# Layer 1 attention: tail steps at new slots, maxima combined behind the last one, low halves of weights later, second batch's projections a tile sooner

## What is computed

```python
qkv = hidden_states @ Wqkv
q = qkv[..., :nH * d].reshape(B, S, nH, d)
k = qkv[..., nH * d:nH * d + d]
v = qkv[..., nH * d + d:]
scores = jnp.einsum('bqhd,bkd->bhqk', q, k) * scale
scores = jnp.where(causal[None, None], scores + alibi[None], NEG_INF)
probs = jax.nn.softmax(scores, axis=-1)
attn = jnp.einsum('bhqk,bkd->bqhd', probs, v).reshape(B, S, H)
return attn @ Wo
...
x = x + _layernorm(_L1_attn_ref(_layernorm(x, axis=-1), L1_attn_Wqkv, L1_attn_Wo), axis=-1)
x = x + _layernorm(_L1_ffn_ref(_layernorm(x, axis=-1), L1_ffn_sign, L1_ffn_scale), axis=-1)
```

## Time and profile before

| | us |
|---|---|
| median of 3 runs (4049.62 to 4056.49) | 4054.41 |
| the profiled execution's own time | 4068.57 |
| its span | 4066.7 |
| PE busy in the span | 3592.4 (88%) |
| DVE busy | 2894.3 (71%) |
| ACT busy | 2362.7 (58%) |
| POOL busy | 2083.7 (51%) |
| mean granted PE clock | 0.956 |

### The profile page before, as it was taken

One profiled execution on the slowest core, in us unless ns is written; L12 is line 12 of the kernel. 1 busy time (PEld: TensorE's weight loads), 2 busy tenths in 40 slices (PEclk: granted clock), 3 DMA queues, 4 the chain that ended last, 5 costly groups with the idle time before them and its releaser, 6 DMA issues.

```text
span 4066.7 us, 62815 instructions
## 1 busy us (share of the span) xinstructions
PE 3592.4 (88%) x21250; PEld 1803.7 (44%) x21250; DVE 2894.3 (71%) x4612; ACT 2362.7 (58%) x4071; POOL 2083.7 (51%) x1710
## 2 busy tenths in 40 slices
PE   3899998899888779999998999999999995776799
PEld 1344443233222345555554555555555553343344
DVE  4544336766674467888888888888888885657787
ACT  4533323555565566676676676666676663455665
POOL 4700000000000347777777877878778776546754
PEclk9999998899898899999999999999999997889999
DMA  3200001000100100000000000000000001012000
GB/s 104 66 10 1 1 21 28 1 7 13 37 8 4 36 18 1 25 13 21 19 8 25 8 26 13 14 25 1 26 13 20 11 1 65 1 52 78 13 11 32
DMA packets 58879, 88.92 MB, mean 22 GB/s; under 512 B 11429, under 2 KB 32440, under 8 KB 58548
## 3 DMA queue, kind: packets, MB, share of 16 engines
q1 hardware_dynamic: 57880, 84.15, 7.2%
q10 hardware_dynamic: 672, 0.59, 0.1%
HBM read 71.05 MB, written 6.85 MB: 19 GB/s over the span
## 4 chain that ended last, share of the span: by engine, by line
PE 62%; DVE 12%; issue 8%; ACT 6%; POOL 4%; SPq 1%; DVEq 0%; ACTq 0%; DMA 0%; POOLq 0%
PE psum L257 12%; PE psum L258 12%; PE psum L259 12%; PE psum L1397 3%; PE psum L1370 2%; PE psum L2495 2%; PE psum L2507 2%; PE psum L2503 2%; PE psum L2464 2%; DVE arena L1563 2%; PE psum L1381 2%; PE psum L3160 1%; PE psum L3161 1%; DVE x L2189 1%; PE psum L2486 1%
## 5 line engine op out<-in xcount | busy, mean ns | idle before, releaser
L257 PE MATMUL psum<-xt_hi,arena 128*128 128x512 f16 (+1 forms) x1920 | 739.4, 385 | 20.8 <-ACT arena L2017 5.9
L258 PE MATMUL psum<-xt_lo,arena 128*128 128x512 f16 (+1 forms) x1920 | 738.1, 384 | 0.0
L259 PE MATMUL psum<-xt_hi,arena 128*128 128x512 f16 (+1 forms) x1920 | 737.0, 384 | 0.0
L2290 POOL TENSOR_TENSOR arena<-arena 128x1024 f16<-128x1024 f16 x256 | 516.2, 2036 | 49.7 <-DVE arena L2101 32.4
L1563 DVE TENSOR_REDUCE arena<-psum 128x1 f32<-128x512 f32 (+3 forms) x608 | 373.5, 656 | 145.0 <-PE psum L1370 143.2
L257 PE MATMUL psum<-arena 128*128 128x512 f16 (+1 forms) x1152 | 420.2, 368 | 58.5 <-DVE arena L2925 25.5
L1512 ACT ACTIVATE arena<-psum 128x512 f32<-128x512 f32 x576 | 320.6, 599 | 244.9 <-PE psum L1381 161.2
L258 PE MATMUL psum<-arena 128*128 128x512 f16 (+1 forms) x1152 | 419.2, 367 | 0.0
L259 PE MATMUL psum<-arena 128*128 128x512 f16 (+1 forms) x1152 | 418.9, 367 | 0.0
L1311 POOL TENSOR_TENSOR rs<-sd,epsc 128x1 f32<-128x1 f32 x15 | 8.1, 540 | 785.0 <-DVE sd L1611 785.0
L2295 POOL TENSOR_TENSOR arena<-arena 128x512 f16<-128x512 f16 x256 | 314.6, 1248 | 4.6 <-PE psum L2475 4.6
(11 more groups left out here) (364 smaller groups left out, 8332.6 us busy)
## 6 DMA issues: line engine op xcount, KB each, us to landing
arena<-m_wi SPq DMA_DIRECT2D x64, 320.0 KB, 2.9
arena<-m_wo SPq DMA_DIRECT2D x32, 256.0 KB, 2.6
arena<-arena SPq DMA_DIRECT2D x90, 64.0 KB
x<-L_attn_x SPq DMA_DIRECT2D x4, 1024.0 KB, 5.2
arena<-gate_wT SPq DMA_DIRECT2D x16, 224.0 KB, 2.5
arena<-up_wT SPq DMA_DIRECT2D x16, 224.0 KB, 2.5
arena<-down_wT SPq DMA_DIRECT2D x14, 256.0 KB, 2.6
out<-x SPq DMA_DIRECT2D x3, 1024.0 KB, 4.6
```

What stands on the lines that cost most here:

```text
L257: nc.tensor.matmul(out, lh, rh, start=start, stop=False)
L258: nc.tensor.matmul(out, lh, rl, start=False, stop=False)
L259: return nc.tensor.matmul(out, ll, rh, start=False, stop=stop)
L2290: nc.gpsimd.tensor_tensor(m4_ar[:, q], heads[q].broadcast_to([P, HG, P]), m4_le.unsqueeze(1).broadcast_to([P, HG, P]), ALU.mult).then_inc( ...
```

## The change

The tail table is dealt out anew: the projection's four parts stand in two slots instead of four, the layer norm of y and the add come earlier, x_scale and x_norm share a slot, and x, hi and lo come two slots earlier than before. The distance from one tail to the next stays at 24 slots at least. DVE combines the halves of the maxima right behind the last maximum, no longer at the row step. DVE's parts of `ffn_weights` and of the pieces come 12 and 8 slots after ACT's. Batch 1's key and first query projections move from position 6 to position 5. Two query projections (0, 1 and 1, 1) are spread wider: 3 slots apart instead of 2, and 2 instead of 1. Position 1's maxima come 6 slots later in the plan.

```diff
--- before.py
+++ after.py
@@ -503,9 +503,9 @@
         SEQ2 = [(0, t) for t in range(TPB)] + [(1, t) for t in (0, 3, 2, 1, 4, 5, 6, 7)]
         POS2 = {b * TPB + t: p for p, (b, t) in enumerate(SEQ2)}
         TAIL2 = (("heads0", 1), ("o0", 2), ("heads1", 4), ("o1", 5), ("turn", 7), ("turn_hi", 8), ("turn_lo", 9),
-                 ("project0", 10), ("project1", 11), ("project2", 12), ("project3", 13), ("y_stats", 14), ("y_sd", 15),
-                 ("y_scale", 16), ("y_norm", 17), ("add", 18), ("x_stats", 19), ("x_sd", 19), ("x_scale", 20), ("x_norm", 21),
-                 ("x", 22), ("hi", 23), ("lo", 24))
+                 ("project0", 10), ("project1", 10), ("project2", 11), ("project3", 11), ("y_stats", 12), ("y_sd", 12),
+                 ("y_scale", 13), ("y_norm", 14), ("add", 14), ("x_stats", 16), ("x_sd", 16), ("x_scale", 18), ("x_norm", 18),
+                 ("x", 20), ("hi", 21), ("lo", 22))
         LEAD2 = 7
         units2 = [8 * (t + 1) for _, t in SEQ2]
         first2 = [sum(units2[:p]) for p in range(NT + 1)]
@@ -522,16 +522,16 @@
             for piece in [("qp", 0, 0, f) for f in range(KT)] + [("kp", 0, 0), ("kp", 0, 1), ("vp", 0)] + of_tile(0):
                 ring.append((-1, piece))
             for f in range(KT):
-                ring.append((first2[1] + 2 * f, ("qp", 0, 1, f)))
+                ring.append((first2[1] + 3 * f, ("qp", 0, 1, f)))
             for p in range(TPB - 1):
-                feed(of_tile(p + 1), first2[p] - LEAD2, units2[p])
+                feed(of_tile(p + 1), first2[p] - (LEAD2 if p else 1), units2[p])
             for i, piece in enumerate([("kp", 1, 0), ("kp", 1, 1)] + [("qp", 1, 0, f) for f in range(KT)]):
-                ring.append((first2[TPB - 2] + 6 * i, piece))
+                ring.append((first2[TPB - 3] + 6 * i, piece))
             last = TPB - 1
             ring.append((first2[last] + 3, ("vp", 1)))
             feed(of_tile(last + 1) + of_tile(last + 2) + of_tile(last + 3), first2[last] - LEAD2, units2[last])
             for f in range(KT):
-                ring.append((first2[last + 1] + f, ("qp", 1, 1, f)))
+                ring.append((first2[last + 1] + 2 * f, ("qp", 1, 1, f)))
             feed(of_tile(last + 4), first2[last + 1] - LEAD2, 4 * LEAD2)
             far = [unit for p in range(last + 5, NT) for unit in of_tile(p)]
             feed(far, first2[last + 1] + 3 * LEAD2, first2[NT - 1] - first2[last + 1] - 4 * LEAD2)
@@ -565,8 +565,12 @@
                         slot3 += 1
                     if p == 13 and i == 0:
                         steps.append(("ffn_weights", 0))
+                    if p == 13 and i == 12:
+                        steps.append(("ffn_weights_low", 0))
                     if p >= EARLY4 and i == 0:
                         steps.append(("piece", p - EARLY4))
+                    if p >= EARLY4 and i == 8:
+                        steps.append(("piece_low", p - EARLY4))
                     while r < len(RING2) and (WHEN2[r] <= now or RING2[r] == ("max", p, RING2[r][-1])):
                         steps.append(("ring", r))
                         r += 1
@@ -596,6 +600,7 @@
                 steps.append(("ffn", n))
                 if n in (LAST3 + 1, LAST3 + 2):
                     steps.append(("piece", NT - EARLY4 + n - LAST3 - 1))
+                    steps.append(("piece_low", NT - EARLY4 + n - LAST3 - 1))
                 if n == LAST3 + 3:
                     steps.append(("dt_weights", 0))
                 for _ in range(2 if n < LAST3 - 2 else len(ahead)):
@@ -1563,6 +1568,10 @@
                         nc.vector.tensor_reduce(a2_mx[:, q % 2, c // 512, h0:h0 + heads],
                                                 bank[:, 0:heads * w].rearrange("p (h c) -> p h c", h=heads), AXX,
                                                 ALU.max).then_inc(a2_md, 1)
+                        if p == DONE2[q] and SEQ2[q][1] > 3:
+                            dve.wait_ge(a2_md, p + 3)
+                            mx = a2_mx[:, q % 2, 0, :]
+                            nc.vector.tensor_tensor(mx, mx, a2_mx[:, q % 2, 1, :], ALU.max).then_inc(a2_mc, 1)
                     elif kind == "vp":
                         dve.wait_ge(a2_ms, p + 1)
                         nc.vector.tensor_scalar(a2_v[piece[0]][:, :, 0:D2],
@@ -1585,10 +1594,6 @@
                         f = piece[2]
                         nc.vector.scalar_tensor_tensor(out=a2_ql[:, f, :], in0=bank, scalar=0.25 / WS, in1=a2_qh[:, f, :],
                                                        op0=ALU.mult, op1=ALU.subtract).then_inc(a2_md, 1)
-                elif what == "row" and SEQ2[p][1] > 3:
-                    dve.wait_ge(a2_md, DONE2[p] + 3)
-                    mx = a2_mx[:, p % 2, 0, :]
-                    nc.vector.tensor_tensor(mx, mx, a2_mx[:, p % 2, 1, :], ALU.max).then_inc(a2_mc, 1)
                 elif what in ("o0", "o1"):
                     half = int(what[-1])
                     dve.wait_ge(a2_at, p * 2 + half + 1)
@@ -1633,9 +1638,9 @@
                     dve.wait_ge(xt_h, p + (NT * (s + 1) + 1))
                     nc.vector.tensor_tensor(xt_lo[:, :, ds(i * P, P)], ps_m.rearrange("p (k c) -> p k c", k=KT),
                                             xt_hi[:, :, ds(i * P, P)], ALU.subtract).then_inc(xt_ok, 1)
-                elif what == "ffn_weights":
+                elif what == "ffn_weights_low":
                     dve_l1_weights(dve)
-                elif what == "piece":
+                elif what == "piece_low":
                     dve_first_piece(dve, p)
                 elif what == "dt_weights":
                     dve_dt_weights(dve)
```

## The result

The changed kernel takes 4048.65 us (median of 20 runs), the kernel before 4056.85 beside it (20 runs): ratio 0.9971, interval [0.9958, 0.9984], about 12 us less (0.29%). 36 us were forecast, in a range of 3992 to 4044. So it is faster, by a third of the forecast, and it lies outside the range.

What follows compares the result with a forecast made beforehand. PE was taken to set the attention stage's pace, losing time to waits and half clock. Waits saved 30.8 us, less 8 replacing them, plus 13 of clock: 36 us off the 4054.4 median, 4018.4 us, range 3992 to 4044.

Steps and rivals of the forecast that it cites:

- Tails, lo: PE's waits for lo at heads0: seven of eight vanish as lo comes two slots earlier, 8.0 us saved.
- y chain: y_stats to x_stats on DVE, POOL and ACT: tighter slots cost 0, with 19 us as upper bound.
- Tails, x: PE's six waits of x for x_norm, 7.9 us: one more slot covers nearly all, 6.9 us saved.
- Combination: PE's eight row-step waits, 12.6 us: combining earlier on DVE removes most of them, 11.0 us saved.
- low halves: Four PE waits behind DVE's low pieces at positions 10 to 12 and 14 go: 5.6 us saved.
- Position 13: The 6.96 us lo wait becomes 4.6: 3.1 for ACT's exponential, 1.5 for DVE's five instructions; 2.4 us saved.
- Projections and ring: Moved projections save 1.4 us net; wider spread costs 2.5 at position 12, position 1's later maxima 2.0.
- What takes their place: Other waits of PE, nearest the ring's 24.6 us for DVE's reductions, grow by 8 us, between 0 and 24.6.
- The clock: Nine half-clock stretches begin at attacked waits; 26.3 us return if all go, half taken: 13 us saved.
- third rival: Removed waits return as PE's waits for DVE's reductions, doubling 24.6 us, no clock returned: 4048 us, chance 0.11.
- only the waits go: First rival: waits of PE go but half-clock stretches stay as many: 4031 us, chance 0.20.
- signs of being wrong: Ring waits doubled, DVE over 1 us a tail behind POOL, or the stage's mean clock staying at 0.91.

Runs made afterwards that it cites:

- nr_x: The changed kernel without its four ring-plan edits, with x_scale a slot earlier and x, hi, lo a slot later: 4043.71 us, 0.9954 of the kernel before.
- tails_only: The kernel before with the new tail table alone, which also starts position 15's feed-forward steps two slots earlier: 4050.94 us, ratio 0.9967.
- low_only: The kernel before with only DVE's low parts of the weights and pieces issued 12 and 8 slots later: 4056.62 us, ratio 0.9981.
- no_ring: The changed kernel with all four ring-plan edits (projections, their spread, position 1's maxima) undone: 4030.16 us, ratio 0.9921 to the kernel before.
- comb_only: The kernel before with only DVE's combination of the maxima's halves moved right behind the last maximum: 4051.06 us, ratio 0.9973.
- nr_again: The changed kernel without its four ring-plan edits, run and profiled a second time unaltered: 4035.62 us, ratio 0.9936 to the kernel before.
- nr_phase: The changed kernel without its ring-plan edits, with position 15's ffn steps back at their old slots: 4026.06 us, ratio 0.9914 to the kernel before.
- nr_both: The changed kernel without ring-plan edits, with both position 15's ffn steps put back and two slots between x_norm and x: 4043.86 us, ratio 0.9948.
- no_first: The changed kernel with position 1's maxima back at their old place in the plan: 4037.09 us, ratio 0.9935 to the kernel before.

## Why the prediction was wrong, step by step

**Tails, lo (-8.0):** right; no lo wait is left. **y chain (0):** near; DVE's waits for POOL are 0.8 us at y_scale (0.7 before) and 8.2 at x_stats (7.8 before).

**Tails, x (-6.9): wrong, +2.2.** The step that failed is "one slot covers all but the rest of the longest", with a slot of 1.25 us. One tail of the changed kernel, on DVE, ACT and PE:

```profile
892.57 0.68 DVE L1568 TENSOR_REDUCE arena<-psum 128x1 f32<-128x512 f32 x1
893.17 0.20 DVE L1634 TENSOR_SCALAR rs<-mv,rs 128x1 f32<-128x1 f32 x1
893.41 0.81 ACT L218 ACTIVATE xn<-x,rs 128x512 f32<-128x512 f32 x1 [1.83 <-DVE rs L1634]
894.28 0.55 PE L1470 MATMUL psum<-ident,xn 128*128 128x128 f32 x3 [0.96 <-ACT xn L218]
```

ACT has been idle for 1.83 us when x_scale comes out of DVE from behind the reductions. With x_scale and x_norm in one slot the chain starts as late as DVE is behind, and the table's slots are not equal: 1.25 us is the mean, and those without projections and tail matmuls are shorter: the two scores just ahead of this x start at 892.10 and 892.94, 0.84 us apart. In the sum this step is off by 9.1 us. nr_x, with one slot more on either side of x_norm, brought these waits to 2.6 us.

**Combination (-11.0), low halves (-5.6):** right in kind; the waits are gone. **Position 13:** a wait for ACT's exponential of 3.19 us, forecast 3.1; DVE's five instructions of weights, forecast at 1.5, are followed by 0.32 us directly and then by 0.95 and 0.23. How much of it is theirs is not shown: tails_only, which has no weights there, has waits of 0.23 and 0.95 in the same position, and low_only, which has them with the old table, has 0.26 behind them. The first of the five and the two larger waits:

```profile
1165.50 2.28 DVE L1662 SCALAR_TENSOR_TENSOR arena<-arena 128x2048 f16<-128x2048 f32 x1
```

```profile
1168.96 0.26 PE L1371 MATMUL psum<-arena 64*128 64x128 f16 x2 [0.32 <-DVE arena L1568]
1170.54 0.26 PE L1371 MATMUL psum<-arena 64*128 64x128 f16 x2 [0.95 <-DVE arena L1568]
```

**Projections and ring (+3.1 together): mis-sized.** Of the single waits one was close, position 1 with 2.25 us (2.0 forecast); position 6 had 3.70 (2.5) and position 12 only 0.70 (3.8), less than the 1.27 of before. The idle time of the four edits is 65.3 - 58.1 = 7.2 us. DMA waits are 2.4 of it (9.7 us against no_ring's 7.3); about 3 are waits of the projections' matmuls and behind projections, and 2.1 the third stage's turn, which the forecast had not seen. The time is more: 32 or 26 us without them, 12 with, so 14 to 20. What remains above the 7 us is clock, at the start of the stage (shown above) and elsewhere.

**What takes their place (+8): near.** Ring waits did not rise but fell by 4.2 us (a net figure, with the 5.6 us of the pieces in it); the waits of and behind projections rose by 4.3 and the third stage's turn by 3.4 instead. With the 5.6 counted apart that is 1.4 + 4.3 + 3.4 = 9.1 us in place of the waits that went, near 8, but most of it not at the reductions. The shift of the ffn steps, which is in no line of the diff, was not foreseen. All in all, the forecast had 33.9 - 8 = 25.9 us of idle time without the ring edits and the runs 22.4; with them 22.8 and 15.3.

**The clock (+13): this step failed.** It read that stretches at half clock begin beside waits, and concluded that without those waits half of them would be gone. Busy time of the stage fell by 3.8 us in the changed kernel, 25.7 in tails_only, 14.2 in comb_only, 19.7 and 13.0 in the two profiles of no_ring, and by 0.7 in nr_x, which has the second lowest idle time. Taken from all runs instead, as the time gained less the idle time gained, what is left for the clock (and the rest of the program) is a gain of 10 us in tails_only, 2 in comb_only, 3 in low_only, 10 and 4 in no_ring and nr_again, and a loss of 3 us in the changed kernel, where the forecast had a gain of 13, and of 7 in nr_x. Over the twelve variants busy time does not follow idle time. A wait can set off a stretch, but how long it stays at half clock (3, 10 or 20 us behind the same waits at position 13) is in part chance and in part depends on something in the order of work that these profiles do not show. What that is stays open. The Trainium skill's page "TensorE: Matmul & The Clock Gate", section "HAM oscillation", by which waits this short cost no clock, would have given 23 us for this case, nearer to the 12 measured; but that is luck, as stretches at half clock stand beside short waits here (behind the 0.95 us at position 13 in the changed kernel, nr_again, nr_phase, nr_x and nr_both), so the rule's reason is not borne out.

**The rest of the program** took 9.6 us more in the changed kernel's profile, with PE busy 7.3 us more on unchanged work. In the other kernels it was between 2706.6 (comb_only) and 2720.7 us (no_first); no_ring had 2715.3 and nr_again, the same kernel, 2711.9. It follows no edit. The forecast took it as fixed; it is an uncertainty of some 7 us either way.

By its number the third rival, "the waits move to DVE's reductions", is nearest (4048 us), but by luck: ring waits did not double, they fell. By its mechanism the first is nearest, "only the waits go", 4031 us; the ring edits' cost and the rest of the program make the difference. Of the signs of being wrong that the forecast named, one came true: the clock's mean stayed at 0.91.

## What to carry to other kernels

Split a stage into PE's idle and busy time before comparing: single waits repeated within 0.5 us between executions and idle time added up within some microseconds from part to part, while busy time ran over 27 us (615.1 to 642.1) among variants that differ by a few slots, in part by chance. A difference of busy time between two single profiles needs the runs beside it, to see how far each profiled execution lies from its median. Forecast idle time by rows, give the clock a range as wide as its whole effect and no sign, and try each part of a bundle alone and left out: here one of four parts cost more than half of what the others brought. A distance in slots is worth the shortest slot, not the mean, and a constant that other code derives (a table's last slot) moves that code too.

## What the runs showed of the hardware

Twice a kernel with less idle time had more of its stage at half clock and came out no faster: nr_x against nr_again (3.6 us less idle; medians 4043.71 and 4035.62 us, granted clock 0.91 and 0.93, busy 640.1 and 627.8 us for the same matmuls) and nr_both against nr_phase (6.2 us less idle; medians 4043.86 and 4026.06 us, clock 0.91 and 0.94, busy 642.1 and 619.7 us). The full clock does not always return soon once PE is busy: at position 13 of nr_x it stayed at 0.50 from 1160 to 1180 us with PE busy 19.8 of 20 us, and nr_both did the same from 1162 to 1182. The same instructions behind the same waits had half clock for 3.4 us in two executions and for 10 in a third (no_ring, nr_again, nr_phase). And of two executions of the same kernel one had 6.7 us more of PE's busy time in the stage at the same idle time.
